# C1's gathered units: the last addition moved from VectorE into TensorE's transposes

## The chip, the cores and the metric

The kernel runs on one core of one Trainium2 chip. The metric is the device time of one execution in microseconds (us); the median of three runs is given, and one further execution was taken with the hardware profiler. Engines are named as the profile names them: PE is TensorE (PEld its weight loads), DVE VectorE, ACT ScalarE, POOL GpSimd, SP SyncE.

## What is computed

The input is 8 images of 32 channels and 80 x 80 pixels. Each is normalised per channel and put through a deformable convolution (L0), and the result is added to the input. The sum is normalised again and put through two more deformable convolutions, C1 and C2, with a residual around them. All three have 9 taps; offsets (and, in C1 and C2, a mask) come from an ordinary 3 x 3 convolution, and every tap is a bilinear sample of four corners. Cut to the part that the change touches, C1:

```python
om1 = conv2d(x, w_om1, b_om1)                 # offsets and mask, 27 channels
o1, o2, m1 = jnp.split(om1, 3, axis=1)
offset1, mask1 = jnp.concatenate([o1, o2], axis=1), jax.nn.sigmoid(m1)
# bilinear_gather: for each tap the four corners, each times its weight
for yi, xi, wgt in corners:
    acc = acc + (wgt * valid) * jnp.take_along_axis(x_flat, idx, axis=3)
samp = acc * mask1
out = jnp.einsum('bckhw,ock->bohw', samp, w_dcn1)
```

## The kernel before

The images are worked as four pairs. A tile is 16 x 16 pixels of the two images of a pair, 25 tiles to a pair, and a tile has four units (`UNITS`): 128 pixels of one image each. Three ways of sampling stand side by side:

- **Gathered tiles.** POOL fetches, for every pixel and tap, a row of 128 numbers (four corners of 32 channels) by an indirect DMA (`gather_tile`, L882), 36 of them to a tile, 9 to a unit, into `G[:, b]`. DVE multiplies them by the weights (`scale`, L2063), adds two halves of the corners in place (`halve`, L2070), and adds the last two into `SUM[:, b % 2]` (`sum_up`, L2077). PE turns `SUM` with three transposes into `RED` (pixels to columns, channels and taps to rows), ACT copies that to `SAMP`, PE projects with the convolution's weights. G has one buffer per unit: POOL waits with unit b of the next tile until `summed` has counted this tile's unit b.
- **Dense tiles** (L0). DVE multiplies windows of the image by nine weights (`weight_window`, L2248), nine products to a unit, and PE adds them with 27 accumulating transposes (three groups of nine, L1107 and L1133).
- **Half strips** of C1 (32 x 2 pixels to each of two images, 64 columns wide). PE makes the samples along x by matmuls (`taps_half`, L1176), DVE weights them along y (`weight_half`, L2163), PE adds them with accumulating transposes in sets of 15 (L1186).

`schedule` writes the order by hand. After the dense tiles of pair 0 alone, C1 of pair p is worked beside L0 of pair p + 1. Three kinds of step hold a gathered tile of C1: the **pair step** (`consume_pair`: a gathered and a dense tile; 36 of them), the **both step** (`consume_both`: a gathered tile and a half strip; 40, of which 16 are pair 3's, with no dense tiles left) and a gathered tile alone (`consume`; 4). They recur as pair step, dense, pair step, both step, dense. Between pairs the next pair's table for the gathers is built and stored. C2, with strips and gathered tiles of its own, follows from about 4489 us on.

Within a pair step DVE does, for each unit, scale, halve, sum, then the nine window products of the dense tile's unit; PE does the turn of the gathered unit (`turn_beside`, L1123), an offset convolution in some places (L1059), the projection of the unit before (L1145), then the 27 transposes of the dense unit (L1133). Unit 1 on DVE is followed by the first part of the next tile's indices (`locate`). At the step's end PE turns the next dense tile's offsets, ACT copies them to `Q`, and DVE makes that tile's weights from Q (L1848 on). Within a both step DVE puts scale, halve and sum between the products of the half strip: the halving follows product 1 and the sum product 3 of a half (of units 0 and 2), and they follow products 6 and 7 for the other two; PE's turns are `turn_unit` (L1195).

Waits that matter: the turn of a unit waits for `summed`; the sum waits for `reduced`, the turn of the unit two before, because SUM has two buffers; the products of the dense tile wait for `prod_used`, PE's reading of the buffer's last contents.

Of the kernel before, what the change touches and what calls it, by code (L numbers as in the profile page):

```python
# [7 lines left out]
B, C, H, W = 8, 32, 80, 80  # L8
# [4 lines left out]
TAPS, GROUPS, TPG = 9, 3, 3  # L13
# [13 lines left out]
UNITS = 4  # L27
# [26 lines left out]
L0, C1, C2 = 0, 1, 2  # L54
# [16 lines left out]
def build_program(nc, x, w_off, b_off, w_dcn, par, ident_d, base_y_d, base_x_d, bbase_d, out):  # L71
# [10 lines left out]
    with ctx:  # L82
# [13 lines left out]
        G = sb("G", [128, UNITS, TAPS, ROW])  # L96
# [25 lines left out]
        def arena(at, n):  # L122
            return ARENA[:, at:at + n]

# [794 lines left out]
        def _(pe):  # L919
            class on:  # L920
# [161 lines left out]
                def consume(step):  # L1082
                    z, m, prep = step.seg.z, step.i, step.prep
                    for b in range(UNITS):
                        if prep and b == 2:
                            on.convolve(*prep)
                        if prep and b == 3:
                            on.turn_offsets(*prep)
                        pe.wait_ge(z.summed, UNITS * m + b + 1 + UNITS)
                        pe.wait_ge(z.samp_ready, step.v + b + 1)  # L1090
                        for gr in range(GROUPS):
                            last = nc.tensor.transpose(RED[b % 2][0:TPG * C, gr * 128:(gr + 1) * 128],
                                                       SUM[:, b % 2, TPG * gr:TPG * (gr + 1), :].rearrange("p k c -> p (k c)"),
                                                       IDENT[:, :])
                        last.then_inc(z.reduced, 1)
# [22 lines left out]

                def turn_beside(step, b):
                    pe.wait_ge(main.summed, UNITS * step.i + b + 1 + UNITS)  # L1120
                    pe.wait_ge(main.samp_ready, step.v + 2 * b + 1)
                    for gr in range(GROUPS):
                        last = nc.tensor.transpose(RED[0][0:TPG * C, gr * 128:(gr + 1) * 128],  # L1123
                                                   SUM[:, b % 2, TPG * gr:TPG * (gr + 1), :].rearrange("p k c -> p (k c)"),
                                                   IDENT[:, :])
                    last.then_inc(main.reduced, 1)
# [64 lines left out]
                def turn_unit(step, b):  # L1191
                    pe.wait_ge(main.summed, UNITS * step.i + b + 1 + UNITS)
                    pe.wait_ge(main.samp_ready, step.v + (1, 3, 5, 6)[b])
                    for gr in range(GROUPS):
                        last = nc.tensor.transpose(RED[0][0:TPG * C, gr * 128:(gr + 1) * 128],  # L1195
                                                   SUM[:, b % 2, TPG * gr:TPG * (gr + 1), :].rearrange("p k c -> p (k c)"),
                                                   IDENT[:, :])
                    last.then_inc(main.reduced, 1)
# [496 lines left out]
        def _(dve):  # L1695
# [12 lines left out]
            class on:  # L1708
# [363 lines left out]

                def sum_up(z, m, b):
                    g = G[:, b]
                    dve.wait_ge(z.halved, UNITS * m + b + 1)
# [63 lines left out]
                def consume(step):  # L2139
# [3 lines left out]
                    for b in range(UNITS):  # L2143
                        on.scale(z, m, step.q, b)
                        on.halve(z, m, b)
                        on.sum_up(z, m, b)
# [22 lines left out]
                def consume_both(step, half):  # L2169
                    m, q = step.i, step.q  # L2170
                    dve.wait_ge(main.prep_v, PREP * step.n)
                    for im in range(2):
# [4 lines left out]
                        on.halve(main, m, b)  # L2177
                        on.weight_half(half, im, 2)
                        on.weight_half(half, im, 3)
                        on.sum_up(main, m, b)  # L2180
# [7 lines left out]
                        on.halve(main, m, b + 1)  # L2188
                        on.weight_half(half, im, 7)
                        on.sum_up(main, m, b + 1)  # L2190
# [27 lines left out]
                def consume_pair(step, dense):  # L2218
                    m, d = step.i, dense.i
                    dve.wait_ge(main.prep_v, PREP * step.n)  # L2220
                    for b in range(UNITS):
# [3 lines left out]
                        on.halve(main, m, b)  # L2225
                        on.sum_up(main, m, b)
# [126 lines left out]
```

## Time and profile before

| | us |
|---|---|
| median of three runs | 6914.19 |
| lowest, highest | 6902.07, 6914.28 |
| profiled execution, device time | 6903.11 |
| its span, first to last instruction | 6901.3 |
| PE busy in the span | 6028.7 (87%) |
| DVE busy | 4828.0 (70%) |
| POOL busy | 4612.9 (67%) |
| ACT busy | 2206.3 (32%) |

The profiled execution is one of its own; the time outside its span is 1.8 us. In the profile a line number stands for all instructions of that line, so L2063 is every scaling. Busy shares are averages over stages with different limits; where the work stands is read from stretches and single steps.

### The profile page before, as it was taken

What the parts mean: (1) busy time and instruction counts of PE and PEld (TensorE: products, weight loads), DVE (VectorE), ACT (ScalarE), POOL (GpSimd) and SP (SyncE); (2) the same over time, 40 slices, a digit from 0 to 9 for tenths busy, and PEclk for the clock granted to TensorE, in tenths of its full rate; (3) what the DMA queues carried; (4) which work ended last, traced back from release to release, by engine and by line L of the source; (5) the groups of instructions that cost most, each with busy time, mean ns of one, the idle gap of its engine ahead of it and who ended that gap; (6) DMA issues with size and microseconds to landing.
All of it is one profiled execution on the core that took longest, in us unless ns stands there. A gap on an engine that the chain in (4) does not pass through costs nothing. (4 is left out here: it accounts for less than half of the span.)

```text
span 6901.3 us, 125469 instructions
## 1 busy us (share of the span) xinstructions
PE 6028.7 (87%) x47333; PEld 4764.8 (69%) x47333; DVE 4828.0 (70%) x11440; ACT 2206.3 (32%) x3376; POOL 4612.9 (67%) x4765
## 2 busy tenths in 40 slices
PE   6987888987888887888977988789999999998996
PEld 6886677766677766676765655567777777776775
DVE  7886787866777866777864555466767776676765
ACT  1222222221222222222222222234444444443442
POOL 0006776656777757777657777767777777777776
PEclk9997998987999988999987888889999999998998
DMA  4323333334333323333322222233334333333333
GB/s 149 99 94 105 99 108 104 109 87 128 95 107 98 116 81 99 95 109 102 110 78 76 76 74 69 82 80 93 88 81 105 91 85 95 96 87 78 97 83 76
DMA packets 364107, 653.44 MB, mean 95 GB/s; under 512 B 112008, under 2 KB 270744, under 8 KB 355608
## 3 DMA queue, kind: packets, MB, share of 16 engines
q0 software_dynamic: 152064, 311.73, 18.3%
q1 hardware_dynamic: 211480, 333.92, 15.8%
q8 instruction: 388, 6.36, 0.4%
q14 instruction: 175, 1.43, 0.1%
HBM read 599.16 MB, written 46.15 MB: 94 GB/s over the span
## 5 line engine op out<-in xcount | busy, mean ns | idle before, releaser
L882 POOL DMA_INDIRECT G<-table,IDX x4752 | 4598.8, 968 | 2243.1 <-issue 1932.7
L2248 DVE TENSOR_TENSOR ARENA<-ARENA,OUT 128x288 f32<-128x288 f32 x2808 | 1055.5, 447 | 76.2 <-PE RED L1107 46.1
L1107 PE MATMUL RED<-IDENT,ARENA 128*96 128x128 f32 x7344 | 899.2, 283 | 88.0 <-DVE ARENA L2248 87.6
L1499 ACT ACTIVATE SAMP<-RED 96x384 f32<-96x384 f32 x688 | 334.5, 486 | 1917.1 <-PE RED L1317 812.9
L2063 DVE TENSOR_TENSOR G<-G,WPS 128x1152 f32<-128x1152 f32 x528 | 711.5, 1348 | 319.1 <-DMA G<-table,IDX 317.7
L1107 PEld LDWEIGHTS RED<-IDENT,ARENA 128*96 128x96 f32 x7344 | 831.8, 131 | 139.9 <-issue 129.2
L1298 PE MATMUL BTP<-PAD,ARENA 80*128 x2304 | 750.4, 449 | 58.2 <-issue 26.9
L1176 PE MATMUL BTP<-X 80*128 80x480 f32 x1248 | 660.2, 648 | 144.0 <-ACT X L1443 77.3
L1059 PE MATMUL OFF<-PAD,ARENA 128*54 128x128 f32 (+1 forms) x10944 | 754.2, 297 | 27.2 <-ACT PAD L1399 15.4
L1059 PEld LDWEIGHTS OFF<-PAD,ARENA 128*54 128x54 f32 (+1 forms) x10944 | 672.3, 135 | 131.3 <-issue 108.4
L1494 ACT ACTIVATE SAMP<-RED 96x384 f32<-96x384 f32 x528 | 256.9, 486 | 1559.0 <-PE RED L1195 695.0
L1298 PEld LDWEIGHTS BTP<-PAD,ARENA 80*128 80x128 f32 x2304 | 400.0, 194 | 185.6 <-issue 95.6
L1176 PEld LDWEIGHTS BTP<-X 80*128 80x128 f32 x1248 | 228.5, 208 | 406.4 <-issue 222.3
L1133 PE MATMUL RED<-IDENT,ARENA 128*96 128x128 f32 x3888 | 497.5, 289 | 0.0
L1307 PE MATMUL RED<-IDENT,ARENA 128*96 128x128 f32 x3840 | 496.5, 277 | 0.0
L1307 PEld LDWEIGHTS RED<-IDENT,ARENA 128*96 128x96 f32 x3840 | 422.8, 127 | 82.9 <-DVE PAD L2056 24.0
L2163 DVE TENSOR_TENSOR ARENA<-BTP,X 128x480 f32<-128x480 f32 x408 | 266.2, 652 | 305.5 <-PE BTP L1176 305.4
L1133 PEld LDWEIGHTS RED<-IDENT,ARENA 128*96 128x96 f32 x3888 | 454.4, 135 | 35.7 <-issue 26.4
L1298 PE MATMUL OUT<-PAD,ARENA 80*128 x1152 | 418.1, 445 | 0.0
L2248 DVE TENSOR_TENSOR ARENA<-ARENA,WPS 128x288 f32<-128x288 f32 x936 | 357.2, 448 | 72.9 <-PE RED L1107 72.9
L2070 DVE TENSOR_TENSOR G<-G 128x576 f32<-128x576 f32 x528 | 398.3, 754 | 6.0
L1473 ACT ACTIVATE OFFS<-OFF,BOFF 54x128 f32<-54x128 f32 (+1 forms) x512 | 184.9, 361 | 622.9 <-PE OFF L1059 479.1
(213 smaller groups left out, 7681.4 us busy)
## 6 DMA issues: line engine op xcount, KB each, us to landing
ARENA<-wtab SPq DMA_DIRECT2D x208, 800.0 KB
G<-table,IDX POOLq DMA_INDIRECT x4752
ARENA<-xo SPq DMA_DIRECT2D x96, 720.0 KB
X<-xo SPq DMA_DIRECT2D x80, 360.0 KB, 3.7
table<-TB SPq DMA_DIRECT2D x64, 384.0 KB, 2.6
X<-x SPq DMA_DIRECT2D x3, 3200.0 KB, 19.9
out<-X SPq DMA_DIRECT2D x20, 320.0 KB
wtab<-TB SPq DMA_DIRECT2D x16, 384.0 KB, 2.7
```

The costliest lines, as they stand in the source:

```text
L882: pool.indirect_dma_start(G[:, b, k, :], None, tables[seg.table], bass.IndirectOffsetOnAxis(ap=IDX[:, q, b * TAPS + k:b * TAPS + k + 1], a ...
L1059: last = nc.tensor.matmul(out_, WOFF[s][:, k, cols], in_, start=(k == 0), stop=(k == TAPS - 1 and not strip))
L1107: last = nc.tensor.matmul(RED[b % 2][0:TPG * C, gr * 128:(gr + 1) * 128], PROD[gr][:, sft, :], IDENT[:, :], start=(sft == 0), stop=(sft == ...
L1133: last = nc.tensor.matmul(RED[1][0:TPG * C, gr * 128:(gr + 1) * 128], PROD[gr][:, sft, :], IDENT[:, :], start=(sft == 0), stop=(sft == 8), ...
L1176: nc.tensor.matmul(TAPS1[p][c % len(TAPS1[p])][:, 0:TAPW1], TX1[p][im][:, k, :], XT1[p][:, im, row:row + WY1, :].rearrange("p w c -> p (w ...
L1298: nc.tensor.matmul(TAP[c % TAPB][:, 0:TAPW], TXB[tt][:, im, k, :], XT[:, bass.ds(bases[k] + (im * H + row) * C, TAPW)], start=True, stop=T ...
L1307: last = nc.tensor.matmul(RED[1][0:TPG * C, gr * 128:(gr + 1) * 128], PRODS[gr][:, w, :], IDENT[:, :], start=(w == 0), stop=(w == WY - 1), ...
L1499: nc.scalar.activation(SAMP[:, x], RED[x][0:TPG * C, 0:GROUPS * 128].rearrange("p (g n) -> p g n", g=GROUPS), ACT.Copy).then_inc(z.samp_re ...
L2063: nc.vector.tensor_tensor(out=slots, in0=slots, in1=WEIGHTS[q][:, b * TAPS:(b + 1) * TAPS, :].rearrange("p k s -> p (k s)").unsqueeze(2).t ...
L2070: nc.vector.tensor_tensor(out=g[:, :, 0:2 * C], in0=g[:, :, 0:2 * C], in1=g[:, :, 2 * C:], op=ALU.add).then_inc(z.halved, 1)
L2163: nc.vector.tensor_tensor(out=PRODS1[p][(6 * half.i + at) % 2][:, :, j * C:(j + 1) * C], in0=TAPS1[p][c % len(TAPS1[p])][:, 0:TAPW1].rearr ...
L2248: last = nc.vector.tensor_tensor(out=PROD[gr][:, :, j * C:(j + 1) * C].rearrange("p (dy dx) c -> p dy dx c", dy=3), in0=win[:, gr:gr + 3, ...
```

## The change

In C1 the two additions after the scaling become one on DVE and one on PE. `part` replaces `halve` and `sum_up`: it does the halving's addition (the same 576 numbers to a partition), but writes the two parts, with the parts outermost, into `PARTS[b % 2]`. `PARTS[0]` is the old `SUM` (its two buffers together), `PARTS[1]` a stretch of `ARENA` that was free at that time. `add_parts` replaces the three transposes of a turn: for each of the three groups it transposes part 0 and then part 1 into the same place of `RED`, the second accumulating, so six transposes instead of three. `part` counts `summed`, and waits for `scaled` and for `reduced` of the unit two before. C2 keeps `halve`, `sum_up` and three transposes.

```diff
+        PARTS = [SUM, arena(1620, 2 * TAPS * C).rearrange("p (s k c) -> p s k c", s=2, k=TAPS)]
...
+                def add_parts(red, b):
+                    for gr in range(GROUPS):
+                        for part in range(2):
+                            last = nc.tensor.matmul(red[0:TPG * C, gr * 128:(gr + 1) * 128],
+                                                    PARTS[b % 2][:, part, TPG * gr:TPG * (gr + 1), :].rearrange("p k c -> p (k c)"),
+                                                    IDENT[:, :], start=(part == 0), stop=(part == 1), is_transpose=True)
+                    last.then_inc(main.reduced, 1)
+
                 def turn_beside(step, b):
                     pe.wait_ge(main.summed, UNITS * step.i + b + 1 + UNITS)
                     pe.wait_ge(main.samp_ready, step.v + 2 * b + 1)
-                    for gr in range(GROUPS):
-                        last = nc.tensor.transpose(RED[0][0:TPG * C, gr * 128:(gr + 1) * 128],
-                                                   SUM[:, b % 2, TPG * gr:TPG * (gr + 1), :].rearrange("p k c -> p (k c)"),
-                                                   IDENT[:, :])
-                    last.then_inc(main.reduced, 1)
+                    on.add_parts(RED[0], b)
...
+                def part(m, b):
+                    g = G[:, b]
+                    dve.wait_ge(main.scaled, UNITS * m + b + 1)
+                    dve.wait_ge(main.reduced, UNITS * m + b + 1)
+                    nc.vector.tensor_tensor(out=PARTS[b % 2][:, :, :, :], in0=g[:, :, 0:2 * C].rearrange("p k (s c) -> p s k c", s=2),
+                                            in1=g[:, :, 2 * C:].rearrange("p k (s c) -> p s k c", s=2), op=ALU.add).then_inc(main.summed, 1)
...
                         on.scale(main, m, q, b)
                         on.weight_half(half, im, 1)
-                        on.halve(main, m, b)
+                        on.part(m, b)
                         on.weight_half(half, im, 2)
                         on.weight_half(half, im, 3)
-                        on.sum_up(main, m, b)
                         on.weight_half(half, im, 4)
...
                         on.scale(main, m, step.q, b)
-                        on.halve(main, m, b)
-                        on.sum_up(main, m, b)
+                        on.part(m, b)
```

`turn_unit` and the turn in `consume` get `add_parts` in the same way. Every line moves with the added code: scale is L2068 after, `part` L2082, the window products L2260, the half strip's products L2178, the transposes of a turn L1127.

DVE in the first two units of a pair step (after the next dense tile's weights, into OUT and WPS), before:

```order
L2063 TENSOR_TENSOR G<-G,WPS 128x1152
L2070 TENSOR_TENSOR G<-G 128x9x64
L2077 TENSOR_TENSOR SUM<-G 128x288
L2248 TENSOR_TENSOR ARENA<-ARENA,OUT 128x9x32 x9
L2063 TENSOR_TENSOR G<-G,WPS 128x1152
L2070 TENSOR_TENSOR G<-G 128x9x64
L2077 TENSOR_TENSOR SUM<-G 128x288
```

and after:

```order
L2068 TENSOR_TENSOR G<-G,WPS 128x1152
L2082 TENSOR_TENSOR SUM<-G 128x576
L2260 TENSOR_TENSOR ARENA<-ARENA,OUT 128x9x32 x9
L2068 TENSOR_TENSOR G<-G,WPS 128x1152
L2082 TENSOR_TENSOR ARENA<-G 128x576
```

One row per unit is gone, and the halving's row writes SUM or ARENA in place of G.

PE around unit 2 of a pair step (ARENA are the window products, OUT the projections, OFF the offset convolution), before:

```order
L1133 MATMUL RED<-IDENT,ARENA 96x128 x27
L1123 MATMUL RED<-IDENT,SUM 96x128 x3
L1145 MATMUL OUT<-SAMP,WDCN 32x128 x6
L1133 MATMUL RED<-IDENT,ARENA 96x128 x27
L1059 MATMUL OFF<-PAD,ARENA 36x128 x18
```

and after:

```order
L1142 MATMUL RED<-IDENT,ARENA 96x128 x27
L1127 MATMUL RED<-IDENT,SUM 96x128 x6
L1154 MATMUL OUT<-SAMP,WDCN 32x128 x6
L1142 MATMUL RED<-IDENT,ARENA 96x128 x27
L1061 MATMUL OFF<-PAD,ARENA 36x128 x18
```

The order on PE is the same; the turn has six rows for three.

DVE at the start of a both step (X and ARENA hold the half strip's products), before:

```order
L2163 TENSOR_TENSOR X<-BTP,X 128x15x32
L2070 TENSOR_TENSOR G<-G 128x9x64
L2163 TENSOR_TENSOR X<-BTP,X 128x15x32
L2163 TENSOR_TENSOR ARENA<-BTP,X 128x15x32
L2077 TENSOR_TENSOR SUM<-G 128x288
L2163 TENSOR_TENSOR ARENA<-BTP,X 128x15x32
L2063 TENSOR_TENSOR G<-G,WPS 128x1152
```

and after:

```order
L2178 TENSOR_TENSOR X<-BTP,X 128x15x32
L2082 TENSOR_TENSOR SUM<-G 128x576
L2178 TENSOR_TENSOR X<-BTP,X 128x15x32
L2178 TENSOR_TENSOR ARENA<-BTP,X 128x15x32 x2
L2068 TENSOR_TENSOR G<-G,WPS 128x1152
```

What counts `summed` stands two products earlier, in the place of the halving.

## Rows read from the trace of the kernel before

**Rows 1.** The page, part 4: chain of waits, shares of the span.

```profile
PE 19%; POOL 10%; issue 4%; DVE 1%; DMA 0%; ACT 0%; POOLq 0%; DVEq 0%; ACTq 0%
```

**Rows 2.** Stretches, pair 0 and pair 3: length, busy (instructions) per engine, clock, DMA share, GB/s.

```profile
core 0: us, PE busy (x) PEld busy (x) DVE busy (x) ACT busy (x) POOL busy (x), PEclk, DMA share, GB/s
586.60:1643.40 1056.80, 892.03 (x7359) 714.73 (x7359) 778.06 (x1918) 275.41 (x502) 728.14 (x754) 0.89 0.37 105
3701.60:4489.00 787.40, 657.27 (x3849) 447.35 (x3849) 406.26 (x798) 212.22 (x311) 599.66 (x617) 0.84 0.29 76
```

**Rows 3.** Stretches: one pair step, one both step, five recurring steps.

```profile
2361.30:2393.30 32.00, 26.21 (x260) 22.43 (x258) 27.82 (x69) 9.82 (x19) 24.31 (x26) 0.95 0.44 131
2153.10:2194.60 41.50, 38.94 (x250) 25.86 (x248) 26.13 (x51) 8.21 (x17) 31.74 (x33) 0.91 0.27 70
586.60:726.30 139.70, 123.27 (x1018) 99.88 (x1018) 108.39 (x269) 35.24 (x66) 106.19 (x110) 0.89 0.37 104
```

**Rows 4.** Timeline of DVE in that pair step: start, us, what [idle before <-releaser].

```profile
2376.58 0.76 DVE L2070 TENSOR_TENSOR G<-G 128x576 f32<-128x576 f32 x1
2377.37 0.46 DVE L2077 TENSOR_TENSOR SUM<-G 128x288 f32<-128x288 f32 x1
2377.75 3.36 DVE L2248 TENSOR_TENSOR ARENA<-ARENA,WPS 128x288 f32<-128x288 f32 x9
...
2391.48 0.22 DVE L1848 TENSOR_SCALAR SIDES<-Q 128x72 f32<-128x72 f32 x1 [3.36 <-ACT Q L1455]
```

**Rows 5.** Timeline of PE in that pair step, from unit 2's turn.

```profile
2377.89 0.53 PE L1123 MATMUL RED<-IDENT,SUM 128*96 128x128 f32 x3 [3.21 <-DVE SUM L2077]
2378.35 1.37 PE L1145 MATMUL OUT<-SAMP,WDCN 96*32 96x128 f32 x12
2379.65 4.49 PE L1133 MATMUL RED<-IDENT,ARENA 128*96 128x128 f32 x27
```

**Rows 6.** POOL's waits from 3640 to 4480: releaser, us in total, times, longest.

```profile
POOL G L882 <- issue: 198.1, 650, 0.3
POOL G L882 <- DVE SUM L2077: 2.4, 8, 0.3
```

**Rows 7.** Groups by line, 586 to 3640: busy us, mean ns | idle before, releasers.

```profile
L882 POOL DMA_INDIRECT G<-table,IDX x2214 | 2132.7, 963 | 921.8 <-issue 660.8 <-DVE SUM L2077 260.8 <-DMA table<-TB 0.3
...
L1133 PE MATMUL RED<-IDENT,ARENA 128*96 128x128 f32 x3888 | 497.5, 289 | 0.0
```

**Rows 8.** Stretches with the granted clock (third number from the end).

```profile
2379.00:2382.40 3.40, 3.40 (x20) 2.88 (x16) 3.37 (x7) 0.49 (x1) 2.49 (x4) 0.50 0.19 47
2382.50:2385.90 3.40, 3.40 (x49) 3.22 (x49) 3.37 (x9) 0.49 (x1) 2.62 (x3) 1.00 0.26 63
2230.00:2240.00 10.00, 8.27 (x93) 7.08 (x91) 9.86 (x21) 3.42 (x7) 7.56 (x9) 1.00 0.39 120
1662.30:1665.60 3.30, 3.30 (x20) 2.75 (x16) 3.30 (x7) 0.49 (x1) 2.38 (x4) 0.50 0.20 51
```

**Rows 9.** Timeline of PE at unit 2 of two other pair steps.

```profile
652.85 0.88 PE L1123 MATMUL RED<-IDENT,SUM 128*96 128x128 f32 x3 [3.28 <-DVE SUM L2077]
653.66 1.92 PE L1145 MATMUL OUT<-SAMP,WDCN 96*32 96x128 f32 x12
655.51 4.69 PE L1133 MATMUL RED<-IDENT,ARENA 128*96 128x128 f32 x27
...
2232.73 0.53 PE L1123 MATMUL RED<-IDENT,SUM 128*96 128x128 f32 x3 [1.73 <-DVE SUM L2077]
2233.20 1.09 PE L1145 MATMUL OUT<-SAMP,WDCN 96*32 96x128 f32 x12
2234.22 3.15 PE L1133 MATMUL RED<-IDENT,ARENA 128*96 128x128 f32 x27
```

**Rows 10.** Timeline of PE in a both step: one accumulating set.

```profile
2163.10 1.80 PE L1186 MATMUL RED<-IDENT,X 128*96 128x128 f32 x15
```

**Rows 11.** Timeline of DVE in the last both step of pair 2.

```profile
3626.06 0.75 DVE L2070 TENSOR_TENSOR G<-G 128x576 f32<-128x576 f32 x1
...
3631.35 0.45 DVE L2077 TENSOR_TENSOR SUM<-G 128x288 f32<-128x288 f32 x1
```

**Rows 12.** Timeline of POOL at the same place.

```profile
3632.58 0.94 POOL L882 DMA_INDIRECT G<-table,IDX  x1 [6.50 <-DVE SUM L2077]
```

More of the change, by code:

```diff
@@ L1090, in consume @@
                         pe.wait_ge(z.samp_ready, step.v + b + 1)
-                        for gr in range(GROUPS):
-                            last = nc.tensor.transpose(RED[b % 2][0:TPG * C, gr * 128:(gr + 1) * 128],
-                                                       SUM[:, b % 2, TPG * gr:TPG * (gr + 1), :].rearrange("p k c -> p (k c)"),
-                                                       IDENT[:, :])
-                        last.then_inc(z.reduced, 1)
+                        if z is main and step.seg.s == C1:
+                            on.add_parts(RED[b % 2], b)
+                        else:
+                            for gr in range(GROUPS):
+                                last = nc.tensor.transpose(RED[b % 2][0:TPG * C, gr * 128:(gr + 1) * 128],
+                                                           SUM[:, b % 2, TPG * gr:TPG * (gr + 1), :].rearrange("p k c -> p (k c)"),
+                                                           IDENT[:, :])
+                            last.then_inc(z.reduced, 1)
                         if b == 2:
@@ L1117, in consume_dense @@
                     on.project_images(step, 1)
+                def add_parts(red, b):
+                    for gr in range(GROUPS):
+                        for part in range(2):
[3 more added lines that the diff above has]
+                    last.then_inc(main.reduced, 1)
                 def turn_beside(step, b):
@@ L1193, in turn_unit @@
                     pe.wait_ge(main.samp_ready, step.v + (1, 3, 5, 6)[b])
[L1194 to L1198, printed above, removed]
+                    on.add_parts(RED[0], b)
                 def project_units(step, units, sampled):
@@ L2144, in consume @@
                         on.scale(z, m, step.q, b)
-                        on.halve(z, m, b)
-                        on.sum_up(z, m, b)
+                        if z is main and seg.s == C1:
+                            on.part(m, b)
+                        else:
+                            on.halve(z, m, b)
+                            on.sum_up(z, m, b)
                         if b == 1:
@@ L2187, in consume_both @@
                         on.weight_half(half, im, 6)
-                        on.halve(main, m, b + 1)
+                        on.part(m, b + 1)
                         on.weight_half(half, im, 7)
-                        on.sum_up(main, m, b + 1)
                         on.weight_half(half, im, 8)
@@ L2224, in consume_pair @@
                         on.scale(main, m, step.q, b)
-                        on.halve(main, m, b)
-                        on.sum_up(main, m, b)
+                        on.part(m, b)
                         if b == 1:
```

5 lines of the change are left out of this document (1 added, 4 removed).

## The prediction

> **What bounds the kernel now.** The page's chain of waits comes first. It covers only the end of the run: its shares, PE 19%, POOL 10%, issue 4% and little else [rows 1], add up to about a third of the span, and that third is the second convolution (C2), which the change leaves alone. The stretch that changes, 586.6 to 4489.0 us, has to be read from its own rows. While the first pair is worked (586.6 to 1643.4) PE is busy 892 of 1057 us, DVE 778 and POOL 728; in the fourth pair (3701.6 to 4489.0) PE falls to 657 of 787 and POOL is at 600 [rows 2].
>
> By single steps: a pair step (a gathered tile and a dense tile together, 36 of them) took 32.0 us with PE busy 26.2 and DVE 27.8; a both step (a gathered tile and a half strip, 40 of them) took 41.5 us with PE busy 38.9 and DVE only 26.1 [rows 3]. So neither engine bounds a pair step alone: they take turns. DVE needs 0.76 us for a halving, 0.46 for a sum, 3.36 for nine window products [rows 4]; after three units of that PE, which had finished unit 1, waits 3.21 us for SUM before the turn of unit 2 [rows 5]. From there PE leads to the end of the step, and DVE in its turn waits 3.36 us for Q [rows 4]. In a both step PE leads nearly throughout. In the fourth pair it is POOL: between 3640 and 4480 its waits for SUM come to 2.4 us in all, the rest is the 0.30 us ahead of each gather [rows 6]; with 0.96 us a gather [rows 7] a tile of 36 takes it 45.6 us.
>
> PE's wait of 3.21 us costs more than itself. Behind it the granted clock is 0.50 for 3.4 us [rows 8], the lower of the two levels (1.2 GHz), and the 27 transposes there take 4.49 us [rows 5] where another tile has 3.15 at full clock [rows 9]. Over the three pairs these transposes sum to 497.5 us in 144 sets of 27 [rows 7], 3.45 each, so some 44 us are lost to the clock in this one line.
>
> **What the change removes, adds and moves.** 80 gathered tiles of 4 units each: 36 pair steps, 40 both steps (24 in pairs 0 to 2, 16 in pair 3), 4 alone.
>
> *DVE, removed:* one sum per unit, 0.46 us and its 0.03 gap. The halving keeps its number of elements; its output now goes to another buffer in runs of 32. Scaling, halving and sum lie on one line of time over elements whatever their patterns, so I take the same 0.76 from both sides.
>
> *PE, added:* three transposes per unit. A set of 3 took 0.53 [rows 9], a set of 15 accumulating ones 1.80 [rows 10], one of 27 3.15 [rows 9]; the slope is (1.80-0.53)/12 = 0.106, or 0.109 by the 27. Three more in the same run cost 0.33 by it; the upper bound is a second set with its own start, 0.53. I take 0.33, since accumulating sets of this shape are in the trace.
>
> *Pair step, without the clock.* By unit 2 DVE has dropped three sums, -1.47. PE has 0.66 more to do by then, of which 0.2 still shows, because a turn there starts when the sum comes and the rest waits for PE anyway; so its wait shrinks to 3.21-1.47-0.2 = 1.5 us. Then PE leads, and units 2 and 3 add 0.66. Net -0.81 us; DVE's wait of 3.36 us for Q covers its own later units. 32 pair steps count (in pair 2 the first four stand behind POOL): -26 us.
>
> *Pair step, the clock.* Steps with so short a wait exist in the trace: five waited 1.62 to 1.80 us before unit 2. One waited 1.73 us [rows 9] and its clock stayed at 1.00; of the five only one fell, to 0.50 [rows 8]. A fall costs (4.49-3.15)+(1.37-1.09) = 1.62 us where it is short [rows 5, 9]; where it begins earlier, turn, projection and transposes take 0.88, 1.92 and 4.69 us, 2.7 too much [rows 9]. 27 steps have the long wait of 3.2 to 3.4 us outside POOL's stretch (the first at 652.85 [rows 9]), 16 with the short fall and 11 with the long: 2.07 us on average. If four in five escape: -45 us. The Trainium skill, "TensorE: Matmul & The Clock Gate", Part 4: PE-mode transpose, says that transposes do not count as a busy TensorE in the way matmuls do; by that rule an engine that mostly transposes would not win its clock back, and the sum would lose this term. The trace disagrees so far: the clock was back at 1.00 by 2382.5 [rows 8], while PE was inside 27 transposes that had begun at 2379.65 [rows 5].
>
> *Both step.* PE leads, so 4 x 0.33 = 1.3 us come onto the path; DVE's four sums less are off it. 21 of the 24 in pairs 0 to 2 count (three lie in POOL's stretch): +27 us. Nothing hides this. The steps of a gathered tile alone trade a sum for three transposes: 0.
>
> *POOL's buffers.* POOL refills a unit of G when `summed` counts it. In a both step the sum stands two products and a wait for PE behind the halving. At the last both step of pair 2 the halving ended at 3626.81 and the sum at 3631.80 [rows 11], and POOL, idle 6.50 us for that sum, began at 3632.58 [rows 12] the row of gathers that runs through pair 3 without a pause [rows 6]. Now the halving itself releases, 5.0 us earlier, and as POOL bounds pair 3 the whole of it moves. POOL also bounds the first steps of pair 2, and that run begins on a release of the same kind: another 5. Together -10 us. The 16 both steps of pair 3 hide their transposes behind POOL; C2 is unchanged.
>
> *New waits.* The halving now waits for `reduced` of the unit two before, where the sum did. Queued behind it on DVE are the products on which PE waits; but that turn is done several us earlier in every kind of step, so it costs 0.
>
> Sum: -26 - 45 + 27 - 10 = -54 us. The profiled execution took 6903.1 us for a span of 6901.3, which gives 6849; it lies 11 us under the median of the three runs, 6914.2, to which I refer the forecast: **6860 us**.
>
> **Rivals.**
> *A, the clock does not come back.* The wait shrinks but PE still falls to the lower level, as after one of the five short waits. Then the -45 is gone, and the turn of unit 2 adds its three transposes at half rate, 0.33 more in 27 steps: -26+27-10+9 = 0, 6914 us. Against it stand four of five tiles and the rise inside transposes; for it, that the 1.5 us is an estimate. The skill's rule named above would end here.
> *B, slower: PE pays a second set.* PE leads the both step and the second half of the pair step, so the price c of three more transposes stands 4 x 21 + 2 x 32 = 148 times on the path. Without the clock the rest of the change gains 32 x 1.47 + 10 = 57 us, so it decides from c = 57/148 = 0.39 us. At c = 0.53 and with the clock as in A: 148 x 0.53 - 57 + 9 = +30, 6944 us. Against it is the slope of the sets of 15 and 27.
> *C, POOL binds sooner.* Five steps that recur (two pair steps, a both step, two dense tiles) took 139.7 us [rows 3], and their three gathered tiles need POOL for 3 x 45.6 = 137. The forecast takes 4 us from such a five, so the short ones end at POOL's pace; longer ones, with another offset convolution in them, give POOL the lead that hides it. If the lead is used up, some 2 us are lost in each of six short fives: -42, 6872 us.
>
> **How the numbers follow.** The forecast with its sizes 0.64, C 0.11, A 0.17, B 0.08. A measurement of this kernel tells about 0.2% apart, 14 us. The forecast and C are faster by more, all but a small tail of 0.01 in which over half of the steps still fall; A lies within, less 0.02 that it may give on the fast side; B beyond on the slow side but for 0.01. That is 0.77 faster, 0.16 same, 0.07 slower. The range: all 27 steps escaping gives -65, and the lower of the two levels at which the three runs lie (6902 to 6914) another -12, so 6838 at the low end; a third of the steps escaping gives -28, a price of 0.4 in place of 0.33 adds 10, and part of A brings the high end to 6902.
>
> **What would show it.** In pair steps: PE's wait before the turn of unit 2 near 1.5 us in place of 3.2, the 27 transposes behind it near 3.15 in place of 4.49, the step near 29.5 us in place of 32.0. In both steps: turns of six near 0.85, the step longer by 1.3. The halving still 0.75 to 0.76. POOL's wait ahead of pair 3's run near 1.5 us in place of 6.5, and pair 3 as long as before. The forecast is wrong if the transposes keep their mean of 3.45, if three more cost over 0.4 us, or if POOL's run for pair 3 starts no earlier.

## The result, and the profile after

The changed kernel takes 6865.55 us, median of four executions (6863.51 to 6872.52), against 6914.23 for the kernel before on the same chip: 0.9933 of it, 95% interval 0.9916 to 0.995, which is 49 us less. The same kernel measured again beside the experiments gave 0.9935 (0.9921 to 0.9949), 6857.53 us against 6901.45. The forecast was 6860, between 6838 and 6902, and faster. The profiled execution took 6863.51 us for a span of 6861.6.

The end of the run has not changed; the chain of waits on the page reads as in [rows 1]:

```profile
PE 19%; POOL 10%; issue 4%; DVE 1%; DMA 0%; ACT 0%; POOLq 0%; DVEq 0%; ACTq 0%
```

The stretches of [rows 2] and [rows 3] in the changed kernel, in this order: pair 0, pair 3, the same pair step, the same both step, the same five steps (length, then busy time of each engine, clock near the end):

```profile
core 0: us, PE busy (x) PEld busy (x) DVE busy (x) ACT busy (x) POOL busy (x), PEclk, DMA share, GB/s
588.10:1621.50 1033.40, 891.84 (x7611) 726.69 (x7611) 742.50 (x1833) 275.75 (x502) 727.92 (x752) 0.91 0.35 107
3652.80:4440.00 787.20, 660.03 (x4053) 458.22 (x4053) 381.38 (x733) 212.30 (x311) 599.07 (x618) 0.88 0.26 76
2332.30:2361.70 29.40, 25.74 (x273) 22.60 (x271) 25.81 (x66) 9.74 (x19) 20.83 (x23) 1.00 0.44 134
2121.10:2163.90 42.80, 39.95 (x262) 26.99 (x261) 24.77 (x47) 8.29 (x17) 32.64 (x34) 0.92 0.26 71
588.10:722.50 134.40, 120.71 (x1052) 99.21 (x1053) 103.33 (x256) 35.29 (x66) 102.13 (x106) 0.94 0.34 106
```

Pair 0 is 23.4 us shorter though PE is as busy as before (891.84 against 892.03 us): more instructions, run at a higher clock. Pair 3 is as long as it was. The pair step went from 32.0 to 29.4 us and its clock from 0.95 to 1.00; the both step from 41.5 to 42.8.

PE at unit 2 of that pair step, beside [rows 5], and DVE beside [rows 4] (start, us, what, idle before and releaser):

```profile
2347.34 0.86 PE L1127 MATMUL RED<-IDENT,SUM 128*96 128x128 f32 x6 [1.82 <-DVE SUM L2082]
2348.14 1.09 PE L1154 MATMUL OUT<-SAMP,WDCN 96*32 96x128 f32 x12
2349.16 3.15 PE L1142 MATMUL RED<-IDENT,ARENA 128*96 128x128 f32 x27
...
2362.99 1.41 PE L1112 MATMUL RED<-IDENT,ARENA 128*96 128x128 f32 x7 [2.02 <-DVE ARENA L2260]
```

```profile
2346.51 0.78 DVE L2082 TENSOR_TENSOR SUM<-G 128x576 f32<-128x576 f32 x1
2347.21 3.36 DVE L2260 TENSOR_TENSOR ARENA<-ARENA,WPS 128x288 f32<-128x288 f32 x9
...
2359.97 0.22 DVE L1853 TENSOR_SCALAR SIDES<-Q 128x72 f32<-128x72 f32 x1 [2.89 <-ACT Q L1460]
```

The wait for the sum is 1.82 us where it was 3.21, the projection 1.09 where it was 1.37, the 27 transposes 3.15 where they were 4.49. The last PE row is the start of the dense tile that follows: PE waits 2.02 us there, and the clock falls to 0.50 behind it (a stretch at this lower clock is called a fall below):

```profile
2363.40:2366.60 3.20, 3.20 (x17) 3.04 (x16) 3.05 (x9) 0.00 (x0) 2.29 (x4) 0.50 0.17 50
```

Over the three pairs the 27 transposes show what [rows 7] showed before:

```profile
L1142 PE MATMUL RED<-IDENT,ARENA 128*96 128x128 f32 x3888 | 457.6, 275 | 0.0
```

They took 40 us less. Of the 36 sets in unit 2, 31 had been over 3.3 us; seven are now (ten in a second trace of the changed kernel).

**Where the 54 us of the first convolution went.** The table adds up the steps' lengths (from one step's first product on DVE to the next one's) and gives the difference to the trace of before, in us. "Pair 3 and alone" are the 16 both steps without dense tiles, less the last, and the four gathered tiles alone. C2 is the rest of the span. The other columns are the experiments below; "again" is the kernel before a second time and shows how far a row moves with nothing changed. A second trace of the changed kernel has -76.5, +34.4, +5.6 and -16.4 in the first four rows, -53.0 for C1 and +6.3 for C2.

| | again | after | change in pair steps only | + early sum | change in both steps only | before + filling | after + filling | one part |
|---|---|---|---|---|---|---|---|---|
| pair steps (36) | +2.2 | -76.0 | -70.7 | -73.1 | -0.7 | -57.0 | -87.9 | -77.3 |
| both steps, pairs 0 to 2 (24) | +0.1 | +33.9 | +4.9 | +7.6 | +24.9 | +2.6 | +37.6 | +9.1 |
| dense tiles beside C1 (42) | -1.3 | +4.4 | +3.7 | +7.3 | -14.8 | +0.6 | -4.9 | +6.0 |
| pair 3 and alone | -0.3 | -16.4 | -2.8 | -13.3 | -18.5 | -0.5 | -19.1 | -15.6 |
| C1 | +0.7 | -54.2 | -64.8 | -71.3 | -9.2 | -54.4 | -74.3 | -77.9 |
| C2 | +8.5 | +13.0 | +4.4 | +2.4 | -1.2 | -2.0 | +12.0 | +8.8 |

C1 lost 54.2 us and C2, which the change does not touch, took 13.0 longer in this execution; C2 is explained in the last section.

### The profile page after: what moved, and what is told of

Read it like the earlier page. It is cut to its first block and busy times, and to the rows that moved or that the text cites. A ratio compares the mean times of both kernels' runs of the same rounds, so it can differ in the third digit from the quotient of the medians.

```text
span 6861.6 us, 127069 instructions
## 1 busy us (share of the span) xinstructions
PE 6065.9 (88%) x48293; PEld 4835.4 (70%) x48293; DVE 4697.9 (68%) x11120; ACT 2208.0 (32%) x3376; POOL 4631.2 (67%) x4765
## 3 DMA queue, kind: packets, MB, share of 16 engines
q0 software_dynamic: 152064, 311.73, 16.4%
## 5 line engine op out<-in xcount | busy, mean ns | idle before, releaser
L2260 DVE TENSOR_TENSOR ARENA<-ARENA,OUT 128x288 f32<-128x288 f32 x2808 | 1055.0, 446 | 94.8 <-PE RED L1112 44.7
L1112 PE MATMUL RED<-IDENT,ARENA 128*96 128x128 f32 x7344 | 903.7, 284 | 86.0 <-DVE ARENA L2260 85.6
L2068 DVE TENSOR_TENSOR G<-G,WPS 128x1152 f32<-128x1152 f32 x528 | 711.3, 1347 | 344.0 <-DMA G<-table,IDX 342.6
L1112 PEld LDWEIGHTS RED<-IDENT,ARENA 128*96 128x96 f32 x7344 | 838.1, 132 | 136.7 <-issue 127.1
L1312 PE MATMUL RED<-IDENT,ARENA 128*96 128x128 f32 x3840 | 498.1, 277 | 0.0
L1312 PEld LDWEIGHTS RED<-IDENT,ARENA 128*96 128x96 f32 x3840 | 424.2, 127 | 83.3 <-DVE PAD L2061 25.4
L2178 DVE TENSOR_TENSOR ARENA<-BTP,X 128x480 f32<-128x480 f32 x408 | 264.1, 653 | 301.9 <-PE BTP L1185 297.7
L1142 PE MATMUL RED<-IDENT,ARENA 128*96 128x128 f32 x3888 | 457.6, 275 | 0.0
L1142 PEld LDWEIGHTS RED<-IDENT,ARENA 128*96 128x96 f32 x3888 | 424.5, 127 | 23.3 <-issue 22.9
L2260 DVE TENSOR_TENSOR ARENA<-ARENA,WPS 128x288 f32<-128x288 f32 x936 | 356.9, 446 | 78.7 <-PE RED L1112 78.7
L1195 PEld LDWEIGHTS RED<-IDENT,ARENA 128*96 128x96 f32 x2520 | 296.1, 132 | 39.9 <-issue 34.5
```

The lines of the kernel that those rows point to most:

```text
L1112: last = nc.tensor.matmul(RED[b % 2][0:TPG * C, gr * 128:(gr + 1) * 128], PROD[gr][:, sft, :], IDENT[:, :], start=(sft == 0), stop=(sft == ...
L1142: last = nc.tensor.matmul(RED[1][0:TPG * C, gr * 128:(gr + 1) * 128], PROD[gr][:, sft, :], IDENT[:, :], start=(sft == 0), stop=(sft == 8), ...
L1195: last = nc.tensor.matmul(RED[1][0:TPG * C, gr * 128:(gr + 1) * 128], PRODS1[half.seg.p][at % 2][:, w, :], IDENT[:, :], start=(w == 0), st ...
L1312: last = nc.tensor.matmul(RED[1][0:TPG * C, gr * 128:(gr + 1) * 128], PRODS[gr][:, w, :], IDENT[:, :], start=(w == 0), stop=(w == WY - 1), ...
L2068: nc.vector.tensor_tensor(out=slots, in0=slots, in1=WEIGHTS[q][:, b * TAPS:(b + 1) * TAPS, :].rearrange("p k s -> p (k s)").unsqueeze(2).t ...
L2178: nc.vector.tensor_tensor(out=PRODS1[p][(6 * half.i + at) % 2][:, :, j * C:(j + 1) * C], in0=TAPS1[p][c % len(TAPS1[p])][:, 0:TAPW1].rearr ...
```

## Experiments

All ratios below are to the kernel before, run on the same chip in the same comparison. Beside the kernels with both parts of the change and filling, and with one part left out, the changed kernel ran again as their measure, and came out as expected, at 0.9935:

> The changed kernel itself, as the measure for the three others on the same chip: 0.993 of the kernel before, as measured first.

### The clock by itself: filling PE's wait in the kernel before

```diff
                 def turn_beside(step, b):
-                    pe.wait_ge(main.summed, UNITS * step.i + b + 1 + UNITS)
                     pe.wait_ge(main.samp_ready, step.v + 2 * b + 1)
+                    for _ in range(24 if b == 2 else 0):
+                        nc.tensor.transpose(RED[0][0:TPG * C, 0:128], IDENT[:, 0:TPG * C], IDENT[:, :])
+                    pe.wait_ge(main.summed, UNITS * step.i + b + 1 + UNITS)
```

> The kernel before, with nothing of the change: in unit 2 of a pair step PE makes 24 transposes of the identity into RED ahead of the turn, in the 3.2 us in which it had waited for SUM; they are overwritten by the turn, no other work is touched. This takes the idle time away and leaves the DVE work, so it prices the clock by itself. Theory (the idle time costs the clock, and transposes as filling keep it): 24 x 0.106 = 2.5 us fit into the wait, PE waits 0.6 us still, the clock stays at 1.00, the 27 transposes behind the turn take 3.15 in place of 4.49 and more; 27 steps x 2.07 = 56 us, less some falls that move to the dense tile behind (some 1 us each in a third of the steps, 10 us): 6914 - 45 = 6869 us, with a mean of 275 ns for the 27 transposes as in the changed kernel. Rival (the clock doesn't hang on this wait, or transposes don't hold it): the clock falls all the same, 6914, or with 24 transposes at half rate running 2 us past the sum's end, 6914 + 27 x 2 = 6968 us.

Measured: 0.9934 (0.992 to 0.9947), 45 us less. PE at unit 2 of the same pair step, and the group of the 27 transposes:

```profile
2338.44 2.78 PE L1122 MATMUL RED<-IDENT 128*96 128x128 f32 x24
2341.75 0.53 PE L1125 MATMUL RED<-IDENT,SUM 128*96 128x128 f32 x3 [0.53 <-DVE SUM L2079]
2342.22 1.09 PE L1147 MATMUL OUT<-SAMP,WDCN 96*32 96x128 f32 x12
2343.24 3.15 PE L1135 MATMUL RED<-IDENT,ARENA 128*96 128x128 f32 x27
...
L1135 PE MATMUL RED<-IDENT,ARENA 128*96 128x128 f32 x3888 | 457.9, 275 | 0.0
```

No set in unit 2 is over 3.3 us any more, and the pair steps lose 57.0 us, though DVE does all its old work and PE 24 transposes more in each. My estimate for the clock in 27 steps was 56. So transposes that compute nothing give as much time as the change: the clock is the larger part of what the change gained. The rival is refuted: in all 36 steps the clock stayed at 1.00 through the 24 transposes, the turn, the projection and the 27 transposes behind them. The rule that the prediction took from the Trainium skill, "TensorE: Matmul & The Clock Gate", Part 4: PE-mode transpose, does not hold here: by it a stretch filled with transposes would not keep the clock.

### The work by itself: the same filling in the changed kernel

```diff
                 def turn_beside(step, b):
                     pe.wait_ge(main.samp_ready, step.v + 2 * b + 1)
+                    for _ in range(14 if b == 2 else 0):
+                        nc.tensor.transpose(RED[0][0:TPG * C, 0:128], IDENT[:, 0:TPG * C], IDENT[:, :])
```

> The changed kernel with 14 transposes of the identity ahead of the turn of unit 2 in a pair step, in the 1.8 to 2.2 us in which PE still waits there for the sum; the turn overwrites them. With the clock kept here as in the kernel before with its filling, the two differ by the removed sum and the added transposes alone. Theory: my base term of 0.81 us x 32 = 26 us shows between these two in the pair steps; the filling itself takes away the falls that the changed kernel still has behind unit 2 (3.4 us of low clock in some 8 steps, 1.7 us each), 8 to 14 us less what moves to the dense tiles, so 6866 - 8 = 6858 on the first chip's scale, 0.992 of before. Rival (the changed kernel's gain was all the clock's, the base is nothing because DVE's wait for Q or another wait takes it): its pair steps are as long as those of the kernel before with the filling, and the time is 0.993 or 0.994 of before.

Measured: 0.9913 (0.99 to 0.9927), where the changed kernel beside it was at 0.9935 (0.9921 to 0.9949). PE, the same pair step:

```profile
2334.32 1.69 PE L1135 MATMUL RED<-IDENT 128*96 128x128 f32 x14
2336.23 0.86 PE L1127 MATMUL RED<-IDENT,SUM 128*96 128x128 f32 x6 [0.22 <-DVE SUM L2084]
```

With the clock at 1.00 behind unit 2 in both, the pair steps stand at -57.0 with the old work and -87.9 with the new: 30.9 us over 36 steps, 0.86 each. The median step gains 0.82, which is the base term of the sum, 0.81 (4.1 us of the 30.9 lie in the first pair step of pair 2, where POOL's release counts as well). The changed kernel itself reaches 76.0 of those 87.9; falls remain in some of its steps, 114 us of low clock in the pair steps against 81 here.

### The change in the pair steps only, with a late and an early sum in the both steps

```diff
                         on.weight_half(half, im, 1)
-                        on.part(m, b)
+                        on.halve_c1(m, b)
                         on.weight_half(half, im, 2)
                         on.weight_half(half, im, 3)
+                        on.sum_c1(m, b)
...
```

`halve_c1` and `sum_c1` are the old halving and sum, the sum into `PARTS[b % 2][:, 0]`; PE turns it with three transposes. Units 1 and 3 have the two around product 7 in the same way. For the early sum `sum_c1` stands directly behind `halve_c1`.

> The change in the 36 pair steps (and the 4 gathered tiles alone) only; the 40 both steps keep the halving, the sum two products later and three transposes to a turn. Theory (the terms of my sum stand apart): the pair steps keep what they gained (76 us over 36 in the trace of the changed kernel), the both steps lose the 1.1 us that they had grown by (20 steps outside POOL's stretches, 22 us), and POOL's buffers are released by the late sum again, which costs the 10 us that the early release had given: 6866 - 22 + 10 = 6854 us. In the trace: turn of a both step 0.53 in place of 0.82, both step 31.9 and 41.6 us as before the change. Rival 1 (the both steps had grown because the faster pair step ahead of them hands over at a worse point, not through their transposes): they stay 1.1 us longer and the late sum costs 10, 6876 us. Rival 2 (the early release is worth nothing, the gathered tiles alone shrank for another reason): 6844 us.

> As pair_only, but the sum of a both step stands directly behind its halving, so that a buffer of G comes free 0.5 us after the halving instead of two products and a wait later. Theory: both steps as short as before the change (-22 us against the changed kernel), early release kept but for 0.5 us at each of two places: 6866 - 22 + 1 = 6845 us, the fastest of these kernels. The difference to pair_only is the release alone: 9 us. Rival 1 (POOL takes the gain back, as in the both steps that follow the second pair step of pairs 1 and 2, which had grown by 8.2 and 5.9 us): the shorter both steps only wait longer for gathers; 22 us shrink to those of pair 0 and the middle of the other pairs, some 10 us, 6857. Rival 2 (four sums of 0.46 us more on DVE in a both step come onto the path): 6866 or more.

Measured on one chip: late sum 0.9928 (0.9914 to 0.9942), 6844.36 us; early sum 0.9912 (0.9899 to 0.9926), 6834.35 us. The theory had said 0.9913 and 0.9900 (6854 and 6845 us beside 6914). The late sum lies between it and rival 1 (0.9945), and its interval just leaves out both; the early sum's interval holds both the theory and its rival 1 (0.9918). The steps tell more. In 22 of the 24 both steps of pairs 0 to 2 the growth is gone (+19.8 us in the changed kernel, -2.5 and -3.5 here), so there it was the three transposes. The step behind the second pair step of pair 1 keeps 6.8 and 7.4 of its 8.2 us with three transposes to a turn, and the one of pair 2 keeps 0.6 and 3.7 of 5.9: these grow because the pair steps ahead are faster and DVE then waits for gathers, which is what rival 1 of either kernel said. (With the pair steps as slow as before, in the next experiment, the two grow by 2.6 and 1.8.) DVE in the step of pair 1, late sum:

```profile
1724.53 1.35 DVE L2076 TENSOR_TENSOR G<-G,WPS 128x1152 f32<-128x1152 f32 x1 [4.36 <-DMA G<-table,IDX]
```

The two kernels differ in the place of the four sums of a both step alone, and by 10.0 us at the medians: that is the price of the release. (In the two traces it is 6.5 us over C1: 10.5 in "pair 3 and alone", of which other rows take 4 back.) DVE and POOL in the last both step of pair 2, first with the late sum, then with the early one (two traces, each with its own times):

```profile
3560.69 0.75 DVE L2104 TENSOR_TENSOR G<-G 128x576 f32<-128x576 f32 x1
3567.45 0.45 DVE L2111 TENSOR_TENSOR SUM<-G 128x288 f32<-128x288 f32 x1
...
3568.68 0.94 POOL L885 DMA_INDIRECT G<-table,IDX  x1 [7.96 <-DVE SUM L2111]
```

```profile
3563.04 0.75 DVE L2104 TENSOR_TENSOR G<-G 128x576 f32<-128x576 f32 x1
3563.82 0.46 DVE L2111 TENSOR_TENSOR SUM<-G 128x288 f32<-128x288 f32 x1
...
3565.06 0.94 POOL L885 DMA_INDIRECT G<-table,IDX  x1 [6.99 <-DVE SUM L2111]
```

From the halving's start to POOL's first gather it is 8.0 us with the late sum and 2.0 with the early one. In the table, "pair 3 and alone" is -2.8 with the one and -13.3 with the other.

### The change in the both steps only

```diff
                 def turn_beside(step, b):
...
-                    on.add_parts(RED[0], b)
+                    on.turn_sum(RED[0], b)
...
                         on.scale(main, m, step.q, b)
-                        on.part(m, b)
+                        on.halve_c1(m, b)
+                        on.sum_c1(m, b)
```

> The change in the 40 both steps and the 4 gathered tiles alone; the 36 pair steps keep halving, sum and three transposes. Theory: 21 both steps at +1.1 us, 22 us, less 10 us of earlier release of POOL's buffers: 6914 + 12 = 6926 us. The pair steps stay at 32 to 33 us, their 27 transposes at a mean of 289 ns. Rival 1 (the early release gives nothing): 6936. Rival 2 (the both steps grow only behind a faster pair step): 6904.

Measured: 1.0005 (0.9996 to 1.0014), 1 us less at the medians, where 12 more were expected. The both steps did grow, by 24.9 us (expected 22), and the early release gave 18.5 (expected 10). What I had not expected is the third row: the 42 dense tiles became 14.8 us shorter, with 111 us at the low clock in place of 153. One of them, in the kernel before, and in this one:

```profile
1400.20:1421.00 20.80, 18.86 (x172) 16.84 (x173) 15.11 (x44) 7.78 (x13) 12.26 (x13) 0.92 0.42 124
```

```profile
1395.80:1415.00 19.20, 17.31 (x172) 15.38 (x173) 15.02 (x44) 7.89 (x13) 11.61 (x13) 1.00 0.44 130
```

The same 172 instructions of PE, 1.6 us less, and the clock at 1.00 in place of 0.92: in the kernel before, a fall of 3.4 us lies in this tile, here it does not. Neither rival said so.

### The kernel before once more

> The kernel before itself, for a second trace of it: how far its steps and its second convolution differ between executions with nothing changed. Theory: steps with the same low clock are alike within 0.1 us; falls of the clock in dense tiles (1.5 us each) move about and make some 10 us over C1; the gathers of C2 differ by 2 to 5 ns each, 4 to 10 us over 1840 of them. Rival: the dense tiles are as in the first trace, and what they lost in the kernel with the change in both steps alone (15 us) is an effect of the change.

Measured: 1.0004 (0.9994 to 1.0013). Ahead of pair 3 nearly every step repeats within 0.1 us, its time at the low clock too: 40 of the 42 dense tiles and 29 of the 36 pair steps; the dense tiles' sum differs by 1.3 us. (In pair 3, at POOL's pace, single steps differ by up to 4.7 us and their sum by 0.3.) The same dense tile:

```profile
1398.70:1419.50 20.80, 18.85 (x172) 16.80 (x173) 15.13 (x45) 7.78 (x13) 12.26 (x13) 0.92 0.39 124
```

So for this kernel my theory failed and the rival holds: its falls hardly wander between executions. That is not so of every kernel. Between the two traces of the changed kernel 12 of the 36 pair steps and 5 of the 42 dense tiles differ by 1.1 to 2.1 us. One such dense tile in the one and in the other:

```profile
1934.10:1951.60 17.50, 16.19 (x152) 15.05 (x153) 14.94 (x45) 3.02 (x8) 13.23 (x15) 0.90 0.32 100
```

```profile
1937.90:1953.80 15.90, 14.62 (x152) 13.64 (x153) 14.80 (x45) 3.02 (x8) 12.06 (x13) 1.00 0.33 106
```

These differences cancel: the sum over the dense tiles differs by 1.2 us between the two. With sums that repeat to 1.3 and 1.2 us in two kernels, the 14.8 us in the dense tiles are an effect of the change in the both steps; a single tile of a single trace would not show it. What in the instruction order decides whether a given wait of PE costs a fall, the runs do not settle.

### PE's half of the addition left out

```diff
-                        for part in range(2):
+                        for part in range(1):
```

> The changed kernel with three transposes to a turn: the second part is not added, so TensorE's share of the addition is left out and VectorE's stays as it is. Theory (PE leads both steps and the second half of pair steps, so that three transposes at 0.29 us are on the path there): 20 both steps x 1.1 = 22 us and 32 pair steps x (0.2 + 2 x 0.29) = 25 us less, 6866 - 47 = 6819, 0.986 of before. Rival 1 (the both steps' growth is given back by the dense tiles behind them, as the kernel with the change in the both steps alone suggests, which came out even with the kernel before): only the pair steps gain, 6841, 0.9895. Rival 2 (POOL's gathers bind once the steps are shorter): some 10 us only, 6856, 0.992.

Measured: 0.9903 (0.9888 to 0.9918), 22.6 us under the changed kernel beside it (6834.94 against 6857.53), where 47 were expected and 25 by rival 1. The table shows which half was right: the both steps in pairs 0 to 2 shrink by 24.8 us, as expected, and the pair steps stay where they were (-77.3 against -76.0, and -76.5 in the second trace of the changed kernel). PE at unit 2 of a pair step, and the group of the 27 transposes:

```profile
2378.13 0.53 PE L1127 MATMUL RED<-IDENT,SUM 128*96 128x128 f32 x3 [2.17 <-DVE SUM L2082]
2378.59 1.89 PE L1154 MATMUL OUT<-SAMP,WDCN 96*32 96x128 f32 x12
2380.41 3.83 PE L1142 MATMUL RED<-IDENT,ARENA 128*96 128x128 f32 x26
...
L1142 PE MATMUL RED<-IDENT,ARENA 128*96 128x128 f32 x3888 | 474.6, 282 | 0.0
```

Three transposes less per turn leave PE idle for longer ahead of unit 2 (2.2 to 2.6 us in most steps, 1.8 to 2.2 in the changed kernel), and 20 of the 36 sets there are slow again, 17 us more in the group. In a pair step PE's added work pays for itself in clock: of the 40 us that the group lost through the change, 23 come without PE's three transposes and 17 only with them. Why rival 1 came near the time is not its own reason: it gave the both steps no gain, and they had all of it.

### Filling every wait behind a pair or a both step

The kernel with the early sum, with 14 filling transposes in unit 2, 13 or 28 at the start of a dense tile behind a pair or a both step, 34 at the start of a both step:

```diff
+                def fill(n):
+                    for _ in range(n):
+                        nc.tensor.transpose(RED[0][0:TPG * C, 0:128], IDENT[:, 0:TPG * C], IDENT[:, :])
...
                 def consume_dense(step):
...
+                        if b == 0:
+                            on.fill({"x": 13, "f": 28}.get(step_before[0], 0))
...
                 def consume_both(step, half):
...
+                    on.fill(34 if step_before[0] == "x" else 0)
```

> The kernel with the change in pair steps and an early sum in both steps, with transposes of the identity as filling wherever PE waits behind a pair or a both step: 14 in unit 2 (wait 2.1 us), 13 at the start of a dense tile behind a pair step (2.0 us), 28 behind a both step (3.8 us), 34 at the start of a both step behind a pair step (4.2 us). No other work is touched. Theory (the clock is lost in these waits, whichever work stands ahead, and a low us costs half of itself where PE leads): in pairs 0 to 2 the low time of 500 us falls by 200, 100 us by PE alone, but the gathers need 137 us to five steps of 138 to 140, so some 40 us show: 0.991 - 0.006 = 0.985 of before, with POOL's pauses ahead of a unit's first gather gone in the short fives. Rival 1 (transposes don't hold the clock in these places, or it falls one place later): 0.991. Rival 2 (the filling runs past the end of the waits): 1.0.

Measured: 0.9873 (0.9858 to 0.9888), where 0.985 was expected. In pairs 0 to 2 the low time in pair steps and dense tiles fell from 368 us before to 86. But DVE now waits for gathers. Its waits for the scaling from 586 to 3640, first the changed kernel, then this one (us in total, times, longest; in this one pair 3 begins at 3604, and 17 of the 120 us lie behind that):

```profile
DVE G L2068 <- DMA G<-table,IDX: 23.0, 14, 5.4
```

```profile
DVE G L2089 <- DMA G<-table,IDX: 120.2, 37, 9.0
```

The trace also showed the 28 transposes in dense tiles where PE had had no wait (16.1 us became 18.8), so I left those out, by `step_before[0] = "f" if half.prep else "d"`:

> The kernel with fillings, without those 28 transposes at the start of a dense tile that stands behind a both step without the next strip's preparation; there PE had no wait, and the fourteen or so tiles had grown from 16.1 to 18.8 us. Theory 1 (PE leads there): nine such tiles in pairs 0 to 2 x 2.7 us = 24 us less, 0.9873 - 0.0035 = 0.984 of before. Theory 2 (the gathers bind; VectorE waited 120 us for them in pairs 0 to 2 with the fillings, 23 us in the changed kernel): where the pair is at the gathers' pace, the 2.7 us only lengthen the next wait; the three or four of the nine that stand late in a pair count, 10 us: 0.986.

Measured: 0.9859 (0.9841 to 0.9877), 6802.05 us, the fastest of all. That is theory 2's figure: the dense tiles gave 25 us (-40.6 to before, from -15.8), the both steps took 15 of them back (+41.1 from +25.9) and the pair steps 5. By DVE's waits for gathers it is now POOL that keeps more of the clock's time from showing; no run here makes the gathers faster to prove it.

## Why the prediction was right

- **Pair steps, work.** Forecast -0.81 us each; -0.86 between the two kernels with filling. The wait ahead of unit 2 went to 1.8 to 2.2 us, not to 1.5, so the 0.2 us of added transposes that I let show there did not; the size of the net gain was right all the same.
- **Pair steps, clock.** Forecast 45 of 56 us, four in five escaping. 24 of 31 slow sets escaped (21 in the second trace), and the group lost 40 us of the 44 to lose. Both terms together: -71 forecast, -76.0 measured. Rival A is refuted by this row alone. The share was partly luck: I had taken it from five waits of 1.62 to 1.80 us, the waits that came were 1.8 to 2.2, and with the 2.2 to 2.6 us of the kernel without PE's half 20 sets were slow.
- **Both steps.** Forecast +27, four times 0.33 in 21 steps. A turn of six is 0.82 to 0.86 us against 0.53, so c is 0.29 to 0.33, and the typical step grew by 0.9 to 1.3. The sum over pairs 0 to 2 is +33.9: two steps, behind the second pair step of pairs 1 and 2, grew by 8.2 and 5.9, and the other 22 by 19.8 together. Rival B, a second set at 0.53, did not occur: six transposes run on as one set.
- **Those two steps are rival C in a place where I had not looked.** DVE and PE in the one of pair 1 (33.9 us before, 42.1 now), and POOL's waits in the 75 us ahead of it:

```profile
1734.97 1.35 DVE L2068 TENSOR_TENSOR G<-G,WPS 128x1152 f32<-128x1152 f32 x1 [5.40 <-DMA G<-table,IDX]
...
1736.95 3.57 PE L1185 MATMUL BTP<-X 80*128 80x480 f32 x4 [3.56 <-DVE X L2178]
...
POOL G L884 <- issue: 18.0, 59, 0.3
```

POOL runs without a wait for a buffer, DVE waits 5.40 us for a gather, PE 3.56 for DVE, and the low clock in this step rises from 4.6 to 13.3 us. At the start of a pair POOL has no lead yet; I had looked for this in the middle, by fives, where the gathers only bind once the clock is kept everywhere (the kernels with all fillings). About 12 us went here, part of it time that the pair steps just ahead had gained: the four steps from the start of pair 1 to the end of this one came out 2.1 us longer than before.
- **POOL's release.** Forecast -10, from two places at 5 us. The two kernels with late and early sum differ by 10.0; in the changed kernel "pair 3 and alone" shrank by 16.4, of which the gathered tiles alone ahead of pairs 2 and 3, the two places, have 4.6 and 6.0. The mark I had named was wrong, though: POOL's wait ahead of pair 3's run did not shrink to 1.5 us.

```profile
3581.07 0.75 DVE L2082 TENSOR_TENSOR SUM<-G 128x576 f32<-128x576 f32 x1
...
3582.60 0.95 POOL L884 DMA_INDIRECT G<-table,IDX  x1 [7.64 <-DVE SUM L2082]
```

The row of gathers ahead of it had moved forward as well, by somewhat more. What tells is POOL's start against the step's first product: 8.9 us behind it before, 3.9 now, 5.0 less, as forecast.
- **Dense tiles.** Forecast: nothing. They took 4.4 us more here: twelve of them grew by 1.1 to 1.6 us, the price of a fall like the one shown above, and nine lost 1.0 us or more.
- **The halving** takes 0.76 us in the median into the new buffers (0.75 to 0.82), as it did in place. The new wait for `reduced` does not show: PE's turn is long done, and all the idle time of DVE ahead of the 320 of them is 5.5 us, as it was ahead of the halvings before.

So C1 came out at -54.2 against the sum's -54 (-53.0 in the second trace), but not each term: pair steps, release and the both steps' own growth were 5 to 6 us better each, and 16 us went to gathers and dense tiles, for which the sum had no term. That the total agrees to the microsecond is partly luck. The medians show 49 and 44 us; the rest of the span, C2, does not repeat as closely, and was 13.0 and 6.3 us longer in the two traces.

## What to carry to other kernels

A wait of TensorE has a price beyond its length, and where two engines take turns, the work taken from the one that is late may be worth less than the clock it brings back: fill the wait with idle work first, which prices the two apart and may be the better change. Moving an addition to TensorE pays where that engine waits and costs its full price where it leads, so decide it for each kind of step; here both kinds in one change gave away a quarter of what the pair steps alone, with an early sum in the others, bring (0.9935 against 0.9912). And a buffer's release is worth costing apart from the operation that carries it: the additions of the both steps, placed one or two products earlier, were worth 10 us.

## What the runs showed of the hardware

- **A sum of falls repeats better than a single one.** Two executions of the kernel before have nearly all their low stretches in the same steps (40 of 42 dense tiles within 0.1 us); two of the changed kernel differ in 12 of 36 pair steps and 5 of 42 dense tiles by 1.1 to 2.1 us each. The sum over the 42 tiles repeats to 1.3 us in both, while variants of the kernel move it by -14.8 and +4.4.
- **Transposes hold the clock** at 1.00 whether they compute something or not (24 of the identity, 0.116 us each, in all 36 pair steps).
- **The time of a gather differs between executions, and C2 with it.** The gathers from 4500 us on, nearly all of C2's, by line (busy us, mean ns; C2 starts at other times in the four, so counts and sums are not of the same part) in the kernel before, the same once more, the changed kernel, and the kernel with the change in the both steps only:

```profile
L882 POOL DMA_INDIRECT G<-table,IDX x1841 | 1787.4, 971 | 598.3 <-issue 551.3 <-DVE SUM L2077 46.9
```

```profile
L882 POOL DMA_INDIRECT G<-table,IDX x1844 | 1796.0, 974 | 599.6 <-issue 553.5 <-DVE SUM L2077 46.2
```

```profile
L884 POOL DMA_INDIRECT G<-table,IDX x1825 | 1781.8, 976 | 563.4 <-issue 548.5 <-DVE SUM L2089 14.9
```

```profile
L885 POOL DMA_INDIRECT G<-table,IDX x1836 | 1779.3, 969 | 596.3 <-issue 549.1 <-DVE SUM L2097 47.2
```

With 971, 974, 976 and 969 ns to a gather, C2 took 0, 8.5, 13.0 and -1.2 us more than in the first trace: some 2 us for each nanosecond, as 1840 gathers one behind the other would make it. All twelve traces lie along that line (969.0 to 977.5 ns, C2 2468 to 2483 us, correlation 0.97), while POOL's idle time between the gathers stays at 599 to 601 us. The executions of one kernel lie 4 to 23 us apart, and this may account for much of it; a comparison of traces is best made by sums over C1 ahead of pair 3. What makes the gathers of one execution slower than those of another stays open.
